# Row blocks of X0 loaded as one overlapping DMA per tile, from rows stored twice, with X0 first and 18 idle products on TensorE

## The reference

```python
def _cin_layer(X0, Xi, W, b):                 # X0: 512 x 39 x 16
    Wr = W.reshape(H, F0_, Fi)                # H = 128
    return jnp.einsum('hjk,bjd,bkd->bhd', Wr, X0, Xi) + b[None, :, None]

X0 = Xi = e                                   # e: the 39 gathered rows of each sample
for W, b in Ws:                               # three layers
    Xi = _cin_layer(X0, Xi, W, b)
    res.append(Xi.sum(axis=2))
z = jnp.concatenate(res, axis=1)
h = jnp.maximum(jnp.concatenate([z, dense_ctx], axis=1) @ W_top1 + b_top1, 0.0)
h = jnp.maximum(h @ W_top2 + b_top2, 0.0)
y = h @ W_top3
```

## Time and profile before

| what | us |
|---|---|
| median of 3 runs | 687.69 (687.46 to 687.9) |
| the profiled execution, its own time | 687.18 |
| its span | 685.4 |
| PE busy | 651.5 (95% of the span) |
| DVE / ACT / POOL busy | 555.4 / 493.8 / 342.5 |
| first matmul of layer 1 of chunk 0 | starts at 38.98 |

### The profile page before, as it was taken

The page is one execution under the profiler, slowest core; times in us unless marked ns, Lnnn a source line. Parts: engine busy times, 40 slices in busy tenths (PEclk is TensorE's granted clock), DMA queues, the critical chain, the costliest instruction groups (busy, mean ns, idle before and its releaser), DMA issues.

```text
span 685.4 us, 13530 instructions
## 1 busy us (share of the span) xinstructions
PE 651.5 (95%) x2498; PEld 455.9 (67%) x2498; DVE 555.4 (81%) x1211; ACT 493.8 (72%) x1645; POOL 342.5 (50%) x335
## 2 busy tenths in 40 slices
PE   0489999999999999999999999999999999999998
PEld 0166777777777777777777777777777777774443
DVE  0558898989898989999998989898989999996000
ACT  2166878787887878787878787887878788985002
POOL 6778484738383847566564738383843333000000
PEclk9999999999999999999999999999999999999999
DMA  6532613131312222130303132322222030001000
GB/s 217 130 101 63 223 39 92 39 88 42 88 42 80 52 60 70 39 86 16 99 22 95 36 87 43 87 43 80 50 61 66 29 87 5 0 17 61 1 0 0
DMA packets 40750, 43.44 MB, mean 63 GB/s; under 512 B 20224, under 2 KB 23680, under 8 KB 40585
## 3 DMA queue, kind: packets, MB, share of 16 engines
q1 hardware_dynamic: 24354, 39.60, 19.4%
q0 software_dynamic: 5120, 1.32, 2.1%
q10 hardware_dynamic: 11239, 2.05, 1.6%
HBM read 41.62 MB, written 1.31 MB: 63 GB/s over the span
## 4 chain that ended last, share of the span: by engine, by line
PE 87%; DVE 4%; issue 3%; POOL 2%; DMA 1%; ACT 1%; DVEq 0%; SPq 0%; ACTq 0%
PE acc L359 14%; PE ya L382 12%; PE ya L383 11%; PE ya L384 11%; PE yd L382 9%; PE yd L384 8%; PE yd L383 8%; PE yd L456 5%; PE misc L366 4%; DVE chain L498 2%; POOL emb L304 2%; PE misc L352 1%; DVE x2t L513 1%; DMA x<-x_rows 1%; PE ya L470 1%
## 5 line engine op out<-in xcount | busy, mean ns | idle before, releaser
L614 ACT ACTIVATE prods<-ya,x0t 128x128 f32<-128x128 f32 x1472 | 442.5, 503 | 103.5 <-PE ya L384 103.1
L498 DVE SCALAR_TENSOR_TENSOR chain<-yd,x0t,chain 128x128 f32<-128x128 f32 x768 | 217.9, 342 | 16.7 <-PE yd L384 16.1
L382 PE MATMUL ya<-w1h,x1h 128*128 128x512 f32 (+1 forms) x384 | 206.5, 538 | 1.9 <-DVE x1l L517 1.9
L233 POOL TENSOR_TENSOR prod<-tiles,x0a 120x512 f32<-120x512 f32 x105 | 137.4, 1308 | 128.7 <-PE acc L359 116.8
L304 POOL DMA_INDIRECT emb<-in_tables,rows x160 | 158.3, 990 | 39.4 <-issue 26.3
L383 PE MATMUL ya<-w1l,x1h 128*128 128x512 f32 (+1 forms) x384 | 148.1, 386 | 0.0
L384 PE MATMUL ya<-w1h,x1l 128*128 128x512 f32 (+1 forms) x384 | 147.7, 385 | 0.0
L513 DVE TENSOR_REDUCE x2t<-prods 128x128 f32<-128x1792 f32 x64 | 129.2, 2018 | 1.5 <-DVE chain L498 0.3
L359 PE MATMUL acc<-prod,w 120*128 120x512 f32 x224 | 116.5, 604 | 0.7 <-POOL prod L233 0.6
L513 DVE TENSOR_REDUCE prods<-prods 128x128 f32<-128x1536 f32 x64 | 111.7, 1745 | 0.0
L382 PE MATMUL yd<-w1h,x1h 128*128 128x512 f32 x256 | 104.4, 408 | 1.6 <-DVE chain L498 0.7
(11 more groups left out here) (61 smaller groups left out, 357.2 us busy)
## 6 DMA issues: line engine op xcount, KB each, us to landing
tiles<-x_rows SPq DMA_DIRECT2D x236, 78.0 KB
x0a<-x_rows SPq DMA_DIRECT2D x45, 80.0 KB
emb<-in_tables,rows POOLq DMA_INDIRECT x160, 2.4
w<-in_w SPq DMA_DIRECT2D x3, 832.0 KB, 10.2
w<-in_w SPq DMA_DIRECT2D x1, 2496.0 KB, 10.8
tiles<-x_rows SPq DMA_DIRECT2D x32, 42.0 KB
x<-x_rows SPq DMA_DIRECT2D x16, 78.0 KB
tiles<-x_rows SPq DMA_DIRECT2D x15, 72.0 KB
```

Source lines behind the costliest of these rows:

```text
L233: engine.tensor_tensor(prod0[:, i % L0_PRODS, :], tiles[:, slot, :], x0a[:, :], ALU.mult).then_inc(prod0_ready, 1)
L382: pe.matmul(out, x1h[:, xs], w1h[:, cols], start=True, stop=False)
L498: dve.scalar_tensor_tensor(out, product, x, run if step else b1[:, :], ALU.mult, ALU.add).then_inc(yd_used, 1)
L614: mm = act.activation(prods[:, :, slot_of(q) + i], ya[(NA * g + k) % YA][:, i * H:(i + 1) * H], ACT.Copy, scale=turned(c)[:, g * F1 + j:g ...
```

## The change

The scratch gets 69 rows for each chunk (`STORE`), in place of 40. ACT stores the rows as before with two DMAs, and SP stores with three more (`store_again`) the first 30 rows again behind row 38, so that row r+39 repeats row r. No shifted block wraps round any more, and tile i is one DMA: its source is an access pattern of three blocks of 40 rows of 512 elements, of which block u starts one row behind block u-1 (`row_blocks(x, 3 * i, 1)`); the blocks overlap. `x0a` is one DMA too, with a block step of 0. All loads from the scratch wait for five stores in place of two (`WRITES`).

For chunk 0 SP issues X0 ahead of its tiles (1, 3, 4, 5, 6), and ACT `x0a` and tiles 0 and 2. For a later chunk SP issues `x0a`, tiles 0 to 5, the three repeated stores of chunk x+1 (they wait for `xt`), X0 of chunk x+1, tile 6. Ahead of chunk 0's `turn_x0` PE gets 18 products of the identity with itself (128x128, into `acc0`, which the first step of layer 0 overwrites). The last gathered column takes field 0 in place of field 38.

```diff
+STORE = F + 3 * FO
+WRITES = 5
+WARM = 18
...
+        def row_blocks(x, row, step):
+            return bass.AP(scratch.tensor, (x * STORE + row) * COLS, [[step * COLS, 3], [COLS, R0], [1, COLS]])
...
         def load_x0a(engine, x):
-            for u in range(3):
-                engine.dma_start(x0a[u * R0:(u + 1) * R0, :], chunk_rows(x)[0:R0, :]).then_inc(x0a_in, 16)
+            engine.dma_start(x0a[:, :], row_blocks(x, 0, 0)).then_inc(x0a_in, 16)
 
         def load_tile(engine, x, i):
             wait_done(engine, prod0_ready, uses_before(i, L0_TILES, x))
-            for row, a, b in segments(i):
-                engine.dma_start(tiles[a:b, i % L0_TILES, :],
-                                 chunk_rows(x)[row:row + b - a, :]).then_inc(tile_in[i % L0_TILES], 16)
+            engine.dma_start(tiles[:, i % L0_TILES, :], row_blocks(x, 3 * i, 1)).then_inc(tile_in[i % L0_TILES], 16)
...
+            def store_again(c):
+                sp.wait_ge(x0_ready, c + 1)
+                for i, rows_of, parts in ((0, slice(0, FT), slice(1, 3)), (0, slice(1, FT), slice(0, 1)),
+                                          (1, slice(0, FO - FT), slice(0, 2))):
+                    store_rows(sp, c, i, F, rows_of, parts)
...
                 for i in range(T0 - 1):
                     load_tile(sp, x, i)
                 if nxt:
+                    store_again(x + 1)
                     load_x0(x + 1)
                 load_tile(sp, x, T0 - 1)
...
-            sp.wait_ge(scratch_in, 2 * 16)
-            load_tile(sp, 0, 0)
+            store_again(0)
             load_x0(0)
-            load_tile(sp, 0, 2)
+            load_tile(sp, 0, 1)
+            load_tile(sp, 0, 3)
             for i in range(L0_TILES, T0):
                 load_tile(sp, 0, i)
+            store_again(1)
             load_x0(1)
             load_layer0(1, True)
...
             lay_out(0)
+
+            for _ in range(WARM):
+                pe.matmul(acc0[:, 0:P], const[:, C_ID:C_ID + P], const[:, C_ID:C_ID + P], start=True, stop=True)
             pe.wait_ge(x0_ready, 1)
             turn_x0(0)
...
             load_x0a(act, 0)
-            for i in range(1, L0_TILES, 2):
+            for i in range(0, L0_TILES, 2):
                 load_tile(act, 0, i)
```

More of the change, by code:

```diff
@@ L41 @@
 T0 = (F // 2 + 1 + 2) // 3
-SEGMENTS = 4
+STORE = F + 3 * FO
+WRITES = 5
+WARM = 18
 FT = P // D
@@ L84, in turn_after @@
     return (2, 1) if prev else (3, 1)
-def segments(i):
-    ends = [F - 3 * i + F * u for u in range(SEGMENTS - 1)]
-    return [((3 * i + a) % F, a, b) for a, b in zip([0] + ends, ends + [K0])]
 def fields_of(q):
@@ L167, in build @@
         h1, h2 = gram[:, 0:4, :], gram[:, 4:6, :]
-        scratch = nc.dram_tensor("x0_rows", (CHUNKS, FP, COLS), F32, kind="Internal").ap()
+        scratch = nc.dram_tensor("x0_rows", (CHUNKS, STORE, COLS), F32, kind="Internal").ap()
         acc0, misc = ps("acc0"), ps("misc")
@@ L213, in w1_part, with store_rows @@
             return slice(i * F // W1_PARTS * H, (i + 1) * F // W1_PARTS * H)
+        def row_blocks(x, row, step):
+            return bass.AP(scratch.tensor, (x * STORE + row) * COLS, [[step * COLS, 3], [COLS, R0], [1, COLS]])
+        def store_rows(engine, c, i, first, rows, parts):
+            base, count, lanes = (c * STORE + first) * COLS, parts.stop - parts.start, slice(rows.start * D, rows.stop * D)
+            out = bass.AP(scratch.tensor, base + (parts.start * FO + i * FT + rows.start) * COLS,
+                          [[CB, lanes.stop - lanes.start], [FO * COLS, count], [1, CB]])
+            engine.dma_start(out, xt[lanes, i, parts.start * CB:parts.stop * CB].rearrange("p (f b) -> p f b", f=count)
+                             ).then_inc(scratch_in, 16)
         def load_x0a(engine, x):
-            for u in range(3):
-                engine.dma_start(x0a[u * R0:(u + 1) * R0, :], chunk_rows(x)[0:R0, :]).then_inc(x0a_in, 16)
+            engine.dma_start(x0a[:, :], row_blocks(x, 0, 0)).then_inc(x0a_in, 16)
         def load_tile(engine, x, i):
             wait_done(engine, prod0_ready, uses_before(i, L0_TILES, x))
-            for row, a, b in segments(i):
-                engine.dma_start(tiles[a:b, i % L0_TILES, :],
-                                 chunk_rows(x)[row:row + b - a, :]).then_inc(tile_in[i % L0_TILES], 16)
+            engine.dma_start(tiles[:, i % L0_TILES, :], row_blocks(x, 3 * i, 1)).then_inc(tile_in[i % L0_TILES], 16)
         def multiply0(engine, x, i):
             if i == 0:
-                engine.wait_ge(x0a_in, 3 * 16 * (x + 1))
+                engine.wait_ge(x0a_in, 16 * (x + 1))
             slot = i % L0_TILES
-            engine.wait_ge(tile_in[slot], 16 * SEGMENTS * (x * len(range(slot, T0, L0_TILES)) + i // L0_TILES + 1))
+            engine.wait_ge(tile_in[slot], 16 * (x * len(range(slot, T0, L0_TILES)) + i // L0_TILES + 1))
             wait_done(engine, l0_done, uses_before(i, L0_PRODS, x))
@@ L242, in load_x0 @@
             def load_x0(x):
-                sp.wait_ge(scratch_in, 2 * 16 * (x + 1))
+                sp.wait_ge(scratch_in, WRITES * 16 * (x + 1))
                 wait_done(sp, x0t_done, x)
                 sp.dma_start(x0[:, :], chunk_rows(x)[0:F, :]).then_inc(x0_in, 16)
+            def store_again(c):
[3 more added lines that the diff above has]
+                    store_rows(sp, c, i, F, rows_of, parts)
             def load_layer0(x, nxt):
-                sp.wait_ge(scratch_in, 2 * 16 * (x + 1))
+                sp.wait_ge(scratch_in, WRITES * 16 * (x + 1))
                 wait_done(sp, prod0_ready, T0 * x)
@@ L569, in evacuate_layout @@
                 act.wait_ge(lay_done, c + 1)
-                wait_done(act, scratch_in, 2 * 16 * c)
+                wait_done(act, scratch_in, WRITES * 16 * c)
                 act.activation(xt[:, 0, :], misc[:, 0:P], ACT.Copy)
@@ L573, in evacuate_layout @@
                 act.wait_ge(x0_ready, c + 1)
[L574 to L578, removed]
+                for i, lanes in enumerate((FT, FO - FT)):
+                    store_rows(act, c, i, 0, slice(0, lanes), slice(0, FI))
             def evacuate_x0t(c):
@@ L640, in _ @@
             evacuate_layout(0)
-            act.wait_ge(scratch_in, 2 * 16)
+            act.wait_ge(scratch_in, WRITES * 16)
             load_x0a(act, 0)
-            for i in range(1, L0_TILES, 2):
+            for i in range(0, L0_TILES, 2):
                 load_tile(act, 0, i)
@@ L703 @@
     starts = np.cumsum([0] + [len(t) for t in tables])
-    field = np.minimum(np.arange(FP), F - 1).reshape(FI, FO).T
+    field = (np.arange(FP) % F).reshape(FI, FO).T
     arrays = {
```

## The result

The changed kernel takes 719.65 us (median of 4 runs, 719.12 to 719.93), the kernel before 687.68: a ratio of 1.046, 95% interval 1.045 to 1.048. The forecast was 714, with a range of 703 to 738. The profiled execution spans 717.3 us against 685.4, so 31.9 us have to be found in the trace; the sum of the prediction had 26.5.

The account below looks back on a forecast made before the run. The prediction took PE, 87% of the chain, to bound the kernel. Its terms 17.6+4.4+2.7+1.8 = 26.5 us, added to the profiled 687.18, gave 713.7; with the median 0.5 above, 714 us, range 703 to 738.

Parts of the forecast that it names:

- Number of engines: Every load from the scratch: runs on 3 DMA engines, since one count must divide both sides; the other bound was 15.
- Start, +17.6: Chunk 0: products wait for eight loads queued on three engines, so layer 0 ends at 54.5 against 36.9, +17.6 us.
- Chunk 1's loads, +4.4: Chunk 1: tile 6 queues behind stores and tiles on three engines, its product at S+36.3 against S+31.9, +4.4 us.
- S: Start of layer 1's first matmul, from which later times count: forecast at 56.6 us, 38.98 before.
- w2, +2.7: Behind chunk 1's tile 6: w2's load delays chunk 2's x0a and tile 0, multiplied S+49.6 against S+46.9 wanted, +2.7 us.
- X0 of chunk 3, +1.8: Chunk 2's loads: X0 of chunk 3 comes at S+68.5, where its turn wants it at S+66.7, +1.8 us.
- Later chunks, 0: Chunks after that: SP's cycle of 33.9 us fits within a chunk's 36.7, so loads are hidden at cost 0.
- L: Price of one 120-row load on three engines: forecast 3.5 us, with 3.85 the limit for hiding loads in later chunks.
- The sign that the prediction set: Inner chunks should remain at 36.7 us; if they exceed 37, the forecast value of L is wrong.
- first rival: All loads: spread over 15 engines or near it, a faster start, 684.9 us, or 683.2 if the clock survives; chance 0.07.
- third: Rival for the start: more than three engines, but losing what X0 wins, within 0.2% of before; chance 0.02.
- second: Rival for inner chunks: L above 3.85, so three engines can't keep pace; 738, 786 or about 829 us; chance 0.12.

## Why the prediction was right, and where it was off

**Number of engines: right**, and exactly: 3 completions for a load, 10 once the rows stand outermost. The rule of the Trainium skill that the prediction cites for this (DMA: Bandwidth & Descriptors, "Why a DMA increments its semaphore by 16 and not by 1") agrees for 3 against 120, which no row of before could show; followed alone, the advice of its "Rules for kernel authors" to coalesce costs 32 us here.

**Start, +17.6: measured 17.0** (55.97 - 38.98). Loads of chunk 0 follow at 3.3 in place of 3.5. The 18 products ended at 24.0, not at 27.3, since they soon ran at a higher pace than 0.23; nothing hangs on it.

**Chunk 1's loads, +4.4: measured 7.9**, the step that failed most. Tile 6's step comes at 95.61, 39.6 after layer 1's first matmul, against 31.7 before (70.70 on PE's timeline, which all differences here go by; the chain of the earlier trace rows has 70.87). X0 was issued at S+30.1, within 0.4 of the forecast S+29.7. But the step "tile 6 landed 1.8 + 3.5 later" took the load to be alone on its engines, and charged `w2` only to what stands behind it in SP's ring. The two ran at once: 7.8 from issue to product. Moving `w2` brings it to 6.0. Nor do the steps ahead of it stall within the forecast 4.4: tile 5's is already 4.7 late. A load makes POOL's first product late (S+11.7, before S+7.0), and from there on it is POOL's own pace of gathers and products that holds PE.

**w2, +2.7: measured 1.7** (107.94 - 95.61 = 12.33 against 10.6). Part of its price had been paid by tile 6. Behind PE's wait for tile 6 the clock is 0.71 and 0.66 up to 101; that costs no more here, since PE would have waited for the product anyway, but with tile 0 on ten engines it shows.

**X0 of chunk 3, +1.8: measured 1.7** (146.67 - 107.94 = 38.73 between first steps of chunks 2 and 3, against 36.99).

**Later chunks, 0: measured 3.6** (591.02 - 146.67 = 444.35 from chunk 3's first step to chunk 15's, against 440.76). The transfers are hidden as the working said, with L at 3.5 as it said and 2.0 to spare. But "hidden" was asked of PE alone. Tile 0 is in time for PE's step and late for POOL, whose product then falls on DVE's split; DVE is late by 0.3, and PE has no slack against it: 0.3 in each of 12 chunks. The kernel with `w2` moved, which has the same loads, shows inner chunks of 36.8 to 37.1 too, and tile 0 on ten engines takes all of it away. The sign that the prediction set, that inner chunks over 37 mean a wrong L, would have misled: they took 37.03 with L right.

The sum is 17.0 + 7.9 + 1.7 + 1.7 + 3.6 = 31.9, all of it. Forecast and result are 5.65 apart, mostly the two terms where a transfer or an engine was taken to run alone; together they are 7.1 too small, and the start and `w2`, 1.6 too large, hide some of it. **The rivals**: the loads do not spread (first, and with it the third), and L stays under 3.85 (second); the kernel with two more loads shows how near that edge was: with 7 us more of loads a chunk takes 41 us. What the first rival promised for fast loads, 684.9 or 683.2, the kernels with ten engines miss as well: 691 to 696. Its early X0 comes, its early products don't, and what a won clock gives is handed back in chunks 1 and 2.

## To carry to other kernels

Before one DMA takes the place of several, count for each on how many engines it may be cut: here the outermost 3 of one side decided, not the 120 partitions of the other, and swapping two dimensions of the access pattern gave back 26 of the 32 us. When you call a transfer hidden, follow its first consumer's engine too: an operation that moves within a chunk may fall on another engine's work, even if the bound engine never waits for the transfer. And before an edit that wins time at the start, look what binds the next stage: here POOL's gathers, and a split held by POOL's product, took the gain back.

## What the chip showed that I had not expected

A two-input operation of DVE in SBUF, 0.55 us in each of the 16 chunks, took up to 1.50 us beside POOL's product or `diag`, and one of 0.28 up to 2.04, though no semaphore stands between them. It goes the other way too: in the two chunks where the split was held by the product, the `diag` behind took 1.04 in place of 0.72. DVE's reductions of `x2t` overlap POOL's product and keep their 2.02 us.

SP's three repeated stores take 1.38 us to issue at 82.08, 2.6 to 3.2 in most inner chunks, and 3.3 to 3.8 in most with two more loads in the chunk; with rows outermost they stay at 1.4 to 1.6. Why, was not tried. And one load of 120 rows takes 0.71 to 0.78 us to issue, 1.33 as ACT's first, against 1.03 for the three loads of 40 rows of `x0a`: the single DMA frees SP by 0.3 us only.
